# Cross attention and a mixture of experts on one core: last additions moved into the output stage, rough pairs in other places, the gates in a tensor of their own

## The reference

```python
def xattn(x, context, Wq, Wk, Wv, Wo, bo):      # 16 heads of 64
    q, k, v = x @ Wq, context @ Wk, context @ Wv    # split into heads
    attn = softmax(einsum('bqhd,bkhd->bhqk', q, k) / 8, axis=-1)
    return einsum('bhqk,bkhd->bqhd', attn, v).reshape(B, Nq, h * dh) @ Wo + bo
def ffn(x, router_w, w1, b1, w2, b2):           # 8 experts, 513 tokens each
    scores = softmax(einsum('bsd,ed->bse', x, router_w), axis=-1)
    gate_vals, sel_idx = top_k(swapaxes(scores, 1, 2), 513)
    h = gelu(tokens[sel_idx] @ w1 + b1, approximate=False)
    return zeros.at[sel_idx].add((h @ w2 + b2) * gate_vals)
x = x + xattn(layernorm(x), ctx_768, Wq, Wk, Wv, Wo, bo)
x = x + ffn(layernorm(x), router_w, w1, b1, w2, b2)
```

## Time and profile before

| | us |
|---|---|
| median of 3 runs (lowest to highest) | 1410.77 (1409.52 to 1411.35) |
| the profiled execution | 1409.77 |
| its span | 1408.0 |
| prologue | 0 to 85.6 |
| attention | 85.6 to 1058.1 |
| output | 1058.1 to 1128.3 |
| experts | 1128.3 to 1408.0 |
| TensorE busy | 1311.3 (93%) |
| VectorE, GpSimd, ScalarE busy | 1022.7, 895.9, 805.8 |

### The profile page before, as it was taken

How to read it: one execution, slowest core, us unless ns; L and a number is a source line. 1 busy time by engine, 2 the same in 40 slices (tenths; PEclk the granted TensorE clock), 3 DMA queues, 4 the chain that set the end, 5 groups by cost and what they waited for, 6 DMA issues and landing times. The chain is left out here.

```text
span 1408.0 us, 24896 instructions
## 1 busy us (share of the span) xinstructions
PE 1311.3 (93%) x8340; PEld 823.3 (58%) x8340; DVE 1022.7 (73%) x1670; ACT 805.8 (57%) x1090; POOL 895.9 (64%) x463
## 2 busy tenths in 40 slices
PE   5999999999999999999999999999989817999995
PEld 4655555555555555555555555554439807999995
DVE  4777877887887877788788778777786585655652
ACT  4546666666665666666666666666563215566652
POOL 2237976886787688678668877978693003455353
PEclk8999999999999999999999999999999857999998
DMA  8540001001001100100100010011306233454322
GB/s 229 186 159 9 16 31 49 17 16 63 17 24 42 32 17 23 56 17 24 53 20 17 24 56 24 16 46 69 116 32 207 81 121 99 128 129 105 93 39 24
DMA packets 75559, 88.83 MB, mean 63 GB/s; under 512 B 10507, under 2 KB 55596, under 8 KB 75436
## 3 DMA queue, kind: packets, MB, share of 16 engines
q1 hardware_dynamic: 68652, 78.32, 17.1%
q0 software_dynamic: 6784, 8.94, 3.9%
HBM read 58.98 MB, written 27.99 MB: 62 GB/s over the span
## 5 line engine op out<-in xcount | busy, mean ns | idle before, releaser
L903 POOL TENSOR_TENSOR acc_p<-acc_p,x_in 128x1024 f32<-128x1024 f32 x192 | 489.3, 2549 | 130.8 <-ACT x_in L1003 124.4
L100 DVE TENSOR_REDUCE mx_part<-ps_m 128x1 f32<-128x512 f32 x552 | 362.9, 685 | 184.0 <-PE ps_m L81 182.0
L1003 ACT ACTIVATE x_in<-ps_s 128x1024 f32<-128x1024 f32 x384 | 380.2, 1023 | 97.0 <-PE ps_s L819 69.9
L831 PE MATMUL ps_o<-x_in,v 128*64 128x512 f32 x1664 | 407.7, 608 | 0.2 <-DMA v<-v_scr 0.2
L808 PE MATMUL ps_s<-q,k 64*128 64x512 f32 x2496 | 386.9, 396 | 0.9 <-ACT x_in L1003 0.9
L808 PEld LDWEIGHTS ps_s<-q,k 64*128 64x128 f32 x2496 | 272.8, 185 | 42.9 <-ACT x_in L1003 6.6
L81 PE MATMUL ps_m<-k,q 64*128 64x512 f32 x736 | 212.3, 455 | 6.6 <-issue 2.2
L831 PEld LDWEIGHTS ps_o<-x_in,v 128*64 128x64 f32 x1664 | 99.8, 136 | 181.8 <-issue 142.2
L81 PEld LDWEIGHTS ps_m<-k,q 64*128 64x128 f32 x736 | 99.9, 184 | 143.6 <-issue 98.4
L903 DVE TENSOR_TENSOR acc_d<-acc_d,x_in 128x1024 f32<-128x1024 f32 x96 | 176.2, 1835 | 5.9 <-ACT x_in L1003 5.5
L675 ACT ACTIVATE kept<-ps_m 128x512 f32<-128x512 f32 x184 | 109.7, 596 | 50.3 <-PE ps_m L81 47.6
(11 more groups left out here) (252 smaller groups left out, 1956.0 us busy)
## 6 DMA issues: line engine op xcount, KB each, us to landing
w_in<-in_w SPq DMA_DIRECT2D x16, 1024.0 KB, 5.0
v_st<-rec_scr SPq DMA_DIRECT2D x64, 128.0 KB, 2.9
o_scr<-v_st SPq DMA_DIRECT2D x32, 256.0 KB, 2.1
v<-v_scr SPq DMA_DIRECT2D x8, 832.0 KB, 5.3
v_scr<-c_in SPq DMA_DIRECT2D x10, 512.0 KB, 3.9
c<-o_scr SPq DMA_DIRECT2D x2, 1792.0 KB, 8.4
x_in<-in_x SPq DMA_DIRECT2D x4, 512.0 KB, 11.4
k<-o_scr SPq DMA_DIRECT2D x1, 2048.0 KB, 8.4
```

What stands on the lines that cost most here:

```text
L100: dve.tensor_reduce(part[:, j // S.MF, j % S.MF:j % S.MF + 1], bank[:, 0:S.MC], AX.X, ALU.max).then_inc(done or G.rough_used[hd], 1)
L831: last = pe.matmul(ps_o[hd * HP:hd * HP + DH, :], v[b][:, s, hd * DH:(hd + 1) * DH], probs[:, g % RING, hd * QC:(hd + 1) * QC], start=(s = ...
L903: eng.tensor_tensor(acc, other, probs[:, (u * KT + t) % RING, :], ALU.add).then_inc(done, 1)
L1003: act.activation(probs[:, g % RING, :], ps_s[:, g % 2, :], ACT.Exp, bias=G.pad_bias[:, 0:1] if s == KT - 1 else 0.0, scale=SCALE).then_inc ...
```

## The change

1. **Start of the prologue.** Wv is loaded in two halves of its columns with a semaphore each (three DMAs per half). ScalarE makes all eight context tiles ahead of both halves of Wv. It makes Wk's high part behind v0 and v1 instead of behind v0.
2. **Middle.** VectorE takes k1's low copy behind the aggregates instead of ahead of the last statistics, and k2's and k3's behind the first four normalised tiles. ScalarE takes the root ahead of v5, v6 and v7. The transposed x uses two banks (`turn_bank`), so that the pairs 0 to 2 can use `ps[2]` and `ps[3]`.
3. **Rough pairs.** Pairs 0, 1, 2 stand behind v10, v11, v12. From pair 3 on the pairs alternate between two pairs of banks and wait for the pair two places ahead. They stand behind v13 to v22 by the table `ROUGH_BEHIND`: twice two of them behind one product (v15, v18). The transposition of the maxima stands ahead of the last three products, in a bank of `BANK_USE`; pairs 15 and 16 are last. SP places `m_row` ahead of the last value store.
4. **End of attention.** VectorE's additions of tiles 11 and 12 and GpSimd's of tile 10 of the last unit are issued in the output stage. The denominators come behind output tile 2 instead of 0, the reciprocal in tile 3 instead of 1, the norm in tile 5 instead of 3.
5. **End of the output stage.** The root of the last two token tiles comes ahead of a copy; the logits of tile 13 come behind the transposition of the last two tiles. The scores are made ahead of the gates; the gates have a tensor of their own, and the wait for their store stands ahead of the first gather in the expert stage.

```diff
-LOADS = (48, 16, 48)
-NPJ = 4
+NPJ, RX = 4, 3
 NC = len(ct)
...
 BANK_USE = ("v0 v1 v2 v3 k0 k1 v4 k2 k3 v5 v6 v7 v8 v9 q0 v10 q1 v11 q2 v12 q3".split()
-            + [f"v{n}" for n in range(13, len(vjobs))])
+            + [f"v{n}" for n in range(13, len(vjobs) - 3)] + ["mx"] + [f"v{n}" for n in range(len(vjobs) - 3, len(vjobs))])
+ROUGH_BEHIND = {13: (3,), 14: (4,), 15: (5, 6), 16: (7,), 17: (8,), 18: (9, 10), 19: (11,), 20: (12,), 21: (13,), 22: (14,)}
+ROUGH_LAST = (15, 16)
...
+def rough_bank(r, hd):
+    return ps[(2 if r < RX or r % 2 == 0 else 0) + hd]
+def turn_bank(j):
+    return ps[j % 4] if j < NC else ps[j % 2]
...
-        load_split(2, "wv")
-        load_split(0, "wk")
+        def load_split(n, w, cols, done):
+            sp.dma_start(w_in[n][:, 0, cols], A[w][0:P, cols]).then_inc(done, 16)
+            sp.dma_start(w_in[n][0:HP, 1, cols], A[w][P:S.DC, cols]).then_inc(done, 16)
+            sp.dma_start(w_in[n][HP:P, 1, cols], A[w][P:S.DC, cols]).then_inc(done, 16)
+        load_split(2, "wv", half0, s_wv[0])
+        load_split(2, "wv", half1, s_wv[1])
+        load_split(0, "wk", slice(0, S.DI), s_w[0])
...
         for kt in range(KT):
+            if kt == KT - 1:
+                sp.wait_ge(s_ones, 9)
+                sp.wait_ge(G.mrow_ready, 1)
+                place_mrow(sp, S, G, 0)
             store_v(kt)
...
                 store_weight(1, G.wq_scr, Q_LO)
-        sp.wait_ge(s_ones, 7)
-        sp.wait_ge(G.mrow_ready, 1)
-        place_mrow(sp, S, G, 0)
...
             stats_of(g)
-        for n in range(2):
-            proj_lo(n)
+        proj_lo(0)
         stats_of(3)
...
             dve.bn_aggr(mv[:, t, :], stats[:, t, :]).then_inc(s_mv, 1)
-        for n in range(2, NPJ):
-            proj_lo(n)
+        proj_lo(1)
         dve.wait_ge(s_std, 1)
...
         normalised(0)
+        proj_lo(2)
+        proj_lo(3)
         normalised(1)
...
                 normalised(g + 2)
+            if g >= 2:
+                rough(g - 2)
             if g >= 1:
                 proj_lo(NPJ + g - 1)
-        rough(0)
+        rough(2)
         proj_lo(NPJ + 3)
-        for r in range(1, MJOBS):
+        for r in range(3, MJOBS):
...
         act.activation(std[:, 0:1], eps[:], ACT.Sqrt).then_inc(s_eps, 1)
-        for j in range(4):
+        for j in range(NC):
             hi(j)
-        weight_hi(2, half0)
-        for j in range(4, 6):
-            hi(j)
-        weight_hi(2, half1)
-        for j in range(6, NC):
-            hi(j)
-        keep_v(0)
-        weight_hi(0, pair0)
-        weight_hi(0, pairs)
-        for n in range(1, 4):
+        weight_hi(2, half0, s_wv[0], 48)
+        weight_hi(2, half1, s_wv[1], 48)
+        for n in range(2):
+            keep_v(n)
+        weight_hi(0, pair0, s_w[0], 48)
+        weight_hi(0, pairs, s_w[0], 48)
+        for n in range(2, 4):
             keep_v(n)
...
         proj_hi(3)
-        for n in range(5, 7):
-            keep_v(n)
         act.wait_ge(s_mv, TT)
...
         act.activation(std[:], mv[:, :, 1], ACT.Sqrt, bias=eps[:, 0:1]).then_inc(s_std, 1)
-        keep_v(7)
-        weight_hi(1, pair0)
+        for n in range(5, 8):
+            keep_v(n)
+        weight_hi(1, pair0, s_w[1], 16)
         for g in range(4):
...
         proj_hi(NPJ + 3)
-        weight_hi(1, pairs)
+        weight_hi(1, pairs, s_w[1], 16)
         for n in range(13, len(vjobs)):
+            if n == len(vjobs) - 3:
+                act.wait_ge(G.maxt_ready, 1)
+                act.activation(G.m_row[:], bank("mx")[0:2 * S.QT, 0:P], ACT.Copy, scale=-1.0).then_inc(G.mrow_ready, 1)
             keep_v(n)
...
                 act.activation(G.d_hi[0][:, 0:S.DIFF], kf[:, 0:S.DIFF], ACT.Copy).then_inc(s_diff_hi, 1)
-        act.wait_ge(G.maxt_ready, 1)
-        act.activation(G.m_row[:], ps[2][0:2 * S.QT, 0:P], ACT.Copy, scale=-1.0).then_inc(G.mrow_ready, 1)
...
             pe.wait_ge(s_sthi, NPJ + unit + 1)
+            if r == RX:
+                pe.wait_ge(s_lo, NTJ)
             for hd in range(2):
-                if r == 0:
-                    pe.wait_ge(s_lo, NC + 6)
-                else:
-                    pe.wait_ge(G.rough_used[hd], r)
-                rough_scores(S, G, pe, ps[hd], 0, hd, unit, j)
+                if r >= 1:
+                    pe.wait_ge(G.rough_used[hd], r if r < RX else r - 1)
+                rough_scores(S, G, pe, rough_bank(r, hd), 0, hd, unit, j)
         for j in range(NC):
...
             values(8 + g)
+            if g >= 2:
+                rough(g - 2)
             if g >= 1:
                 proj(NPJ + g - 1)
-        rough(0)
         values(12)
+        rough(2)
         proj(NPJ + 3)
-        rough(1)
         for n in range(13, len(vjobs)):
+            if n == len(vjobs) - 3:
+                pe.wait_ge(G.max_ready, 1)
+                bank_free(pe, "mx")
+                pe.transpose(bank("mx")[0:2 * S.QT, 0:P], G.mx[:], ident[:]).then_inc(G.maxt_ready, 1)
             values(n)
-            rough(n - 11)
-        pe.wait_ge(G.max_ready, 1)
-        pe.wait_ge(s_lo, NTJ)
-        pe.transpose(ps[2][0:2 * S.QT, 0:P], G.mx[:], ident[:]).then_inc(G.maxt_ready, 1)
-        for r in range(len(vjobs) - 11, MJOBS + MAHEAD):
+            for r in ROUGH_BEHIND.get(n, ()):
+                rough(r)
+        for r in ROUGH_LAST:
             rough(r)
...
-        if s - 1 in DVE_TILES[2:]:
+        if s - 1 in DVE_TILES[2:] and not (last and u == UNITS - 1 and s - 1 == DVE_TILES[-2]):
...
-            add_tile(pool, k, u, unit, p * SLOTS + u * KT)
+            if not (last and u == UNITS - 1 and k == NPL - 1):
+                add_tile(pool, k, u, unit, p * SLOTS + u * KT)
...
+G.last_dve_tile = lambda dve, k: add_tile(dve, k, UNITS - 1, NP * UNITS - 1, NP * SLOTS - KT, dve=True)
+G.last_pool_tile = lambda pool: add_tile(pool, NPL - 1, UNITS - 1, NP * UNITS - 1, NP * SLOTS - KT)
+G.last_dve_tiles = (ND - 2, ND - 1)
...
-        add_tile(dve, ND - 1, UNITS - 1, NP * UNITS - 1, NP * SLOTS - KT, dve=True)
...
-        sp.wait_ge(softmax, 5)
-        sp.dma_start(tv[:, :, D:D + E], xn[:, :, D:D + E]).then_inc(table_stored, 16)
         sp.wait_ge(x1_stored, 16 * NB)
-        sp.wait_ge(table_stored, 16 * NB + 16)
+        sp.wait_ge(table_stored, 16 * NB)
+        sp.wait_ge(softmax, 7)
+        sp.dma_start(tv[:, :, D:D + E], G.gates[:]).then_inc(G.gates_stored, 16)
     @block.gpsimd
     def _(pool):
+        G.last_pool_tile(pool)
...
-        for n, (t0, t1) in enumerate(NORM):
+        def root(n):
+            t0, t1 = NORM[n]
             act.wait_ge(mv_done, t1)
             act.activation(std[:, t0:t1], mv[:, t0:t1, 1], ACT.Sqrt, bias=eps[:, 0:1]).then_inc(std_done, 1)
+        for n in range(len(NORM)):
+            if n < NB:
+                root(n)
+            if n == NB - 1:
+                root(n + 1)
...
+        for k in G.last_dve_tiles:
+            G.last_dve_tile(dve, k)
         lo(1, 0)
...
                     lo(1, 1)
-                if t == 1:
+                if t == BT - 1:
                     G.last_dve_rec(dve)
-                if t == BT - 1:
+                if t == BT + 1:
...
-        dve.tensor_tensor(xn[:, :, D:D + E], lg[:], lrec[:, :, None].to_broadcast([P, TT, E]), ALU.mult).then_inc(softmax, 1)
+        dve.wait_ge(softmax, 5)
         dve.tensor_tensor(G.scores[:], lg[:].rearrange("p t e -> p e t"), lrec[:, None, :].to_broadcast([P, E, TT]),
                           ALU.mult).then_inc(softmax, 1)
+        dve.tensor_tensor(G.gates[:], lg[:], lrec[:, :, None].to_broadcast([P, TT, E]), ALU.mult).then_inc(softmax, 1)
...
-                if t == 0:
+                if t == 2:
...
-        for n in range(NB - 1, len(NORM)):
-            transposes(n)
-            logits(n)
+        transposes(NB - 1)
+        pe.wait_ge(t_copied, NB)
+        logits_of(NORM[NB - 1][0])
+        transposes(NB)
+        logits_of(NORM[NB - 1][0] + 1).then_inc(logits_ready, 1)
+        logits(NB)
...
+        pool.wait_ge(G.gates_stored, 16)
...
+    G.x_in = lasting("x_in", [P, S.TT, S.D], F32)
-        G.x_in = sb("x_in", [P, S.TT, S.D], F32)
```

61 lines of the change are left out of this document (31 added, 30 removed).

## The result

The changed kernel took 1397.38 us (median of 4 runs, 1394.2 to 1399.06), the kernel before, on the same chip, 1410.5: a ratio of 0.9901, 95% interval 0.9888 to 0.9913. The forecast was 1399.3, with a range from 1394.5 to 1404.0 that holds the time. The profiled execution took 1399.06 with a span of 1397.3, which is 10.7 less than the 1408.0 of before; the medians differ by 13.1.

A forecast was written before the change was run, and what follows sets the result against it. TensorE was taken to bound attention (busy 960.9 of 968.1 us), so gains lay in waits before and behind it: 6.9 + 2.0 + 0.4 + 2.2 = 11.5 off 1409.77, plus 1.0 for the median, gave 1399.3 us, range 1394.5 to 1404.

The forecast's parts named there:

- prologue and attention, net: Prologue: attention starts 7.6 us earlier, 0.7 given back to a low clock; net 6.9 us, bounds 4.2 and 8.5.
- end of attention and output, with 0.4 at its end: Border into the output stage and its first block: 2.0 us gained, plus 0.4 at the output stage's end.
- gates: End of output stage: the gates' store is no longer waited for; 2.2 us gained, bounds 1.6 and 2.4.
- the tail behind it: Behind the last value product: copy, store and landing unchanged in kind at 4.75 us, perhaps 5.2 with a store backlog.
- the 0.7 set aside for attention's clock: Start of attention: TensorE idles 4 us ahead of it and starts at the low clock, giving back 0.7 us.
- Start: Start of prologue: Wv's first half lands early, so the first value product starts at 16.2 instead of 20.91, 4.7 us earlier.
- Middle: Middle of prologue: two shorter waits ahead of v5 and v7; first transposition of x at 34.05 instead of 38.92.
- Loop: Value products and rough pairs: turns of 1.69 instead of 1.84 us; 38.9 us from first transposition to last product, before 42.0.
- The doubled pairs add no work, they only move: Loop of value products: the doubled rough pairs cost nothing extra; VectorE needs 1.29 us a pair and isn't the bound.
- Rival C: Attention: GpSimd's additions all settle above 3.5 us and set the time, slower at 1415 to 1435 us; chance 0.03.
- End of attention: Output stage starts 4.1 us sooner, but about 3 us of waiting for small loads follows; 2.0 taken, bounds 0.5 and 4.1.
- rival A: First output block: small loads come early, transposition 6.3 us earlier instead of 2.8, total 1395.8 us; chance 0.13.

The follow-up runs named there:

- u_wv: Changed kernel with Wv loaded in one go again, both halves waiting for all three DMAs; 1389.4 us, 0.9916 of the kernel before.
- u_pairs: Changed kernel with one rough pair behind each of v13 to v25, all in one pair of banks; 1388.6 us, 0.9917 of the kernel before.
- n_small: Changed kernel with the loads of router_w and b1 issued ahead of block 2's 2 MB of o_scr; 1390.7 us, 0.9891 of the kernel before.
- a_again: The changed kernel unedited, run again beside other experiments on another chip; 1386.9 us, 0.9906 of the kernel before.
- a_third: The changed kernel unedited, run a third time, in five rounds; 1396.4 us, 0.9908 of the kernel before.
- n_x: Changed kernel with the first two of the four loads of x issued ahead of Wk's three; 1396.9 us, 0.9914 of the kernel before.
- n_three_b: Changed kernel with small loads first, VectorE's low copies reordered and GpSimd's gates wait two memsets earlier, second run; 1394.4 us, 0.9895 of the kernel before.
- second group: One of three groups of four follow-up runs, each on one chip; the kernel before took 1400.1 us here, 1406.2 in the first, 1410.8 in the third.

## Why the prediction was right, and where it wasn't

| step | predicted | profile |
|---|---|---|
| v0 starts | 16.2 | 14.71 |
| first transposition of x | 34.05 | 35.29 |
| last value product ends | 72.95 | 74.8 |
| attention starts | 77.9 to 78.3 | 78.65 |
| prologue and attention, net | 6.9 | 7.0 |
| end of attention and output, with 0.4 at its end | 2.4 | 2.26 |
| gates | 2.2 | 2.3 |
| experts | 0 | -0.9 |
| sum | 11.5 | 10.7 |

That the prologue's 6.9 was met within 0.1 is in part luck: v0 came 1.5 us sooner than predicted, the transposition 1.2 later, the loop took 0.6 more, the tail behind it 0.9 less, and the 0.7 set aside for attention's clock was not needed. The prediction also has a slip: 72.95 and 4.75 to 5.2 give 77.7 to 78.15, not 77.9 to 78.3.

**Start.** Wv's half landed when it was expected; the step that failed is the subtraction, priced at 2.65 by a row in which GpSimd ran beside it. Alone it takes 1.23 (also in u_wv). v0 was 6.2 us earlier, not 4.7.

**Middle.** Waits ahead of v5 and v7 of 1.7 and 1 us were foreseen, with the clock high. There were 2.9 us of waits, ahead of k3 and v5, and the clock fell. Two things were mis-sized: k0's low copy was given by ScalarE's work from v0 on, where x's landing and the statistics set it; its 25.5 was met (25.58), but for another reason, and the earlier v0 brought nothing more. And the clock: in this one profile the transposition came 2.0 us later (14.63 against 12.65 us behind the first statistic), with the clock low from 28.0 to 34.8. In six further traces (u_pairs among them) of the same prologue up to here it stayed high; they had no wait, or one of at most 0.52 us, ahead of k3. The profiled execution (1399.06) is the highest of its four, 1.7 above their median, and this loss may be most of that; no other of the four has a profile, so this is argued, not shown.

**Loop.** 38.9 us were predicted from the first transposition to the end of the last product, 39.5 measured. A turn was to take 1.69; it takes 1.80 with free banks. A product is 1.14 alone where 1.1 was reckoned, a pair 0.43, and the change between them costs 0.23 where 0.16 was reckoned. "The doubled pairs add no work, they only move" was right, but I gave the gain to the banks; by u_pairs it lies for the most part in the maxima being ready and in the last products standing together. The tail behind the last product was 3.9 us, not 4.75.

**Attention.** The 0.7 us for a low clock at its start weren't given back: the clock is low for 3.4 us there in both kernels (79.2 to 82.6, before 86.6 to 90.0), and the stage took 967.45 us between the same two points, 967.43 before. Rival C is out: one of GpSimd's additions takes 2.38 us in both kernels (median), and GpSimd was busy for 746.9 us where it was 749.0.

**End of attention.** 4.1 at the border and a wait for the small loads were predicted, each as it came (2.47 us for "about 3", the small transposes 4.8 earlier for 4.5), and n_small confirms the reason, against rival A: b1's load, issued 0.97 us behind the 2 MB, let TensorE go 7.5 us after its issue, 0.45 behind the large one's landing (1055.01). Rival A's price was wrong too: with the small loads there in time, n_small transposes 24.10 us into the stage, as the kernel before did, so A would be 4.1 us earlier, not 6.3. The low half and the normalised tiles were taken for the bound; they were 0.29 us behind TensorE, whose own order set it, and the low clock behind the wait, for which the 2.0 held back 0.8, cost 1.6. The two errors nearly cancel, and that 2.26 came out near 2.4 is in part luck.

**Gates.** 2.3 for 2.2. That the added wait costs 0.65 us at the first gather was not seen; of b2's load I had allowed 0.3, and it held up nothing (the first count stands 2.74 us behind the transposition of the scores, as before).

## What to carry to other kernels

Find for each wait the last of all its suppliers before pricing what comes from speeding up one of them: the first product came 6 us sooner, and the transposition behind it stood by another input's landing. When work is moved over a stage's border, look at what the next stage waits for in its first microseconds; half of this gain was lost to two small loads queued behind a large one, and moving them by one place brought 2 us back. A wait that is long satisfied can still cost (0.65 us here) if it stands right ahead of the instruction that others are waiting for; put it a few instructions sooner.

## What I had not expected of the hardware

- VectorE's subtraction of Wv's half took 1.23 us alone and 2.65 us where GpSimd's had begun 0.77 us ahead of it. GpSimd's took 2.34 to 2.38 both ways and ended at 19.77; 1.57 us from VectorE's start to there and 1.23 alone are 2.80, near the 2.65. In the same way the two additions at 1047.11 (4.77 us) are 2.37 us until GpSimd's 2.42 ended, and two of 1.2. The Trainium skill, SBUF — State Buffer, on the shared port pair, has the later of two such operations blocked whole; by that rule, the trace agrees. I had cited it and priced the subtraction by the blocked row all the same.
- A wait of 2.5 to 2.9 us ahead of the small transposes was followed by some 3.4 us at the low clock in a_again and by about 6 us in u_wv. In the middle of the prologue, one wait of 1.2 to 1.6 us, with none above 0.52 beside it, left the clock high in six traces; 1.36 and 1.57 us with 1.2 us of work between them were followed by the low clock in one.
- Late in attention the clock was low for 6.8 us in the kernel before and seven others, for 3.4 in the first profile and u_wv, and not at all in u_pairs, a_third, n_x and n_three_b. From its first score product to the end of its last value product the stage took 965.7 to 966.9 us in those four and 967.1 to 968.7 in the others, with nearly the same work in it. That is as much as most of the edits here are worth.
- A satisfied semaphore wait right ahead of GpSimd's indirect gather delayed it by 0.65 us, in ten traces out of ten.
- In the same prologue the landing of x varied from 18.8 to 21.2 us, and the time from the first product of the experts to the end was 224 to 225 us in the second group, 229 to 231 in the first and 232 to 234 in the third: most of what sets the three chips apart.
